# Last stage of a decoder layer: experts' residual through TensorE instead of through memory, and a new order of its small steps

## The reference, cut to what matters

```python
ff = h @ fc2_w + fc2_b                       # h = gelu(x @ fc1_w + fc1_b)
x = layernorm(x + ff, ln3_g, ln3_b)          # inside the cross-attention block
x = _layernorm(x_block_input + x)            # outer norm, called X4 below
# _L0_ffn_ref: tokens 0..15 of each sequence have an expert each, the others share one
xe = x[:, :16, :]
h = gelu(einsum('bnd,ndh->bnh', layernorm(xe, g_e, b_e), W1_e) + b1_e)
out_e = einsum('bnh,nhk->bnk', h, W2_e) + b2_e
out_s = gelu(layernorm(x[:, 16:, :], g_s, b_s) @ W1_s + b1_s) @ W2_s + b2_s
x = _layernorm(x + concatenate([out_e, out_s], axis=1))
```

## Time and profile before

| | us |
|---|---|
| median of 3 runs | 508.43 |
| lowest, highest | 505.97, 509.84 |
| the profiled execution, its own time | 509.53 |
| its span in the trace | 507.7 |
| TensorE, VectorE, ScalarE, POOL busy | 471.4, 384.4, 368.0, 252.4 |
| granted TensorE clock, mean over the span | 0.988 of full |

### The profile page before, as it was taken

One profiled execution on the slowest core, in us unless ns is written; L12 is line 12 of the kernel. 1 busy time (PEld: TensorE's weight loads), 2 busy tenths in 40 slices (PEclk: granted clock), 3 DMA queues, 4 the chain that ended last, 5 costly groups with the idle time before them and its releaser, 6 DMA issues.

```text
span 507.7 us, 14097 instructions
## 1 busy us (share of the span) xinstructions
PE 471.4 (93%) x4644; PEld 432.8 (85%) x4644; DVE 384.4 (76%) x1852; ACT 368.0 (72%) x1390; POOL 252.4 (50%) x342
## 2 busy tenths in 40 slices
PE   3779789999998989999999999999999999999894
PEld 3668788999998989999999999999999997798672
DVE  4667768888888887788878787777777777538866
ACT  4447886868688887777778887777777777836763
POOL 1453366656565665455444455554445545633432
PEclk9899999999999999999999999999999999999987
DMA  8740000000000004000000000000000000400003
GB/s 234 249 175 3 1 3 2 1 3 3 1 2 2 1 3 111 14 2 3 2 2 2 2 2 1 3 1 1 3 1 4 1 2 3 167 1 0 7 16 85
DMA packets 15720, 14.18 MB, mean 28 GB/s; under 512 B 2848, under 2 KB 13344, under 8 KB 15520
## 3 DMA queue, kind: packets, MB, share of 16 engines
q1 hardware_dynamic: 14080, 12.81, 8.0%
q10 hardware_dynamic: 1568, 0.47, 0.5%
HBM read 12.10 MB, written 1.18 MB: 26 GB/s over the span
## 4 chain that ended last, share of the span: by engine, by line
PE 77%; DVE 12%; issue 3%; POOL 2%; ACT 2%; DMA 2%; SPq 1%; POOLq 0%; DVEq 0%; ACTq 0%
PE late_bank L582 11%; PE late_bank L566 11%; PE late_bank L551 11%; PE late_bank L534 11%; PE late_bank L72 9%; PE late_bank L74 9%; PE late_bank L73 9%; DMA x<-in_xT 2%; DVE ffstats L1250 2%; PE late_bank L591 1%; DVE P L1078 1%; ACT P L817 1%; DVE N L1287 1%; PE late_bank L608 1%; DVE at_PT L1104 1%
## 5 line engine op out<-in xcount | busy, mean ns | idle before, releaser
L817 ACT ACTIVATE P<-P,at_negmax 128x128 f32<-128x128 f32 x512 | 199.8, 400 | 81.8 <-DVE at_negmax L1078 81.8
L1519 POOL TENSOR_TENSOR P<-P,at_inv 128x512 f32<-128x512 f32 x128 | 136.6, 1078 | 128.5 <-DVE at_inv L1088 128.4
L1104 DVE COPY at_PT<-late_bank 128x512 f32<-128x512 f32 x128 | 87.8, 688 | 36.0 <-PE late_bank L534 35.7
L1078 DVE CUSTOM_DVE_ANT_0 P<-late_bank,maskb 128x128 f32<-128x128 f32 x512 | 111.2, 286 | 1.8 <-PE late_bank L551 1.7
L817 ACT ACTIVATION_READ_ACCUMULATOR P<-P,at_negmax 128x1 f32 x512 | 101.9, 199 | 0.0
L534 PE MATMUL late_bank<-ident,P 128*128 128x128 f32 x512 | 76.4, 273 | 3.6 <-DVE at_negmax L1078 2.8
L534 PEld LDWEIGHTS late_bank<-ident,P 128*128 128x128 f32 x512 | 59.7, 140 | 9.8 <-issue 5.0
L551 PE MATMUL late_bank<-at_k,at_q 64*128 64x128 f32 x1024 | 65.8, 278 | 0.9 <-DVE at_k L1096 0.9
L551 PEld LDWEIGHTS late_bank<-at_k,at_q 64*128 64x128 f32 x1024 | 59.7, 188 | 4.8 <-issue 1.2
L566 PE MATMUL late_bank<-at_PT,V 128*64 128x128 f32 x1024 | 63.0, 276 | 0.0
L566 PEld LDWEIGHTS late_bank<-at_PT,V 128*64 128x64 f32 x1024 | 55.2, 137 | 3.9
(11 more groups left out here) (195 smaller groups left out, 1055.8 us busy)
## 6 DMA issues: line engine op xcount, KB each, us to landing
ctxT_raw<-in_ctxT SPq DMA_DIRECT2D x1, 1024.0 KB, 8.8
out<-xres SPq DMA_DIRECT2D x4, 224.0 KB, 2.5
x<-in_xT SPq DMA_DIRECT2D x1, 768.0 KB, 9.4
xres<-in_x SPq DMA_DIRECT2D x1, 768.0 KB, 13.6
tap_rows<-in_short_wT SPq DMA_DIRECT2D x3, 192.0 KB, 4.1
sa_wq_raw<-in_sa_wq SPq DMA_DIRECT2D x1, 512.0 KB, 8.0
sa_wk_raw<-in_sa_wk SPq DMA_DIRECT2D x1, 512.0 KB, 9.0
sa_wv_raw<-in_sa_wv SPq DMA_DIRECT2D x1, 512.0 KB, 9.8
```

The lines of the kernel that those rows point to most:

```text
L817: last = nc.scalar.activation(P[:, n % 2, h, :], P[:, n % 2, h, :], ACT.Exp, scale=-1.0, bias=negmax[:, n % 2, h:h + 1], accum_out=total[: ...
L1078: last = nc.vector.tensor_tensor_reduce(P[:, n % 2, h, :], score_bank(h), k.maskb[:, cols(n)], scale=1.0, scalar=3.0e38, op0=ALU.add, op1= ...
L1104: nc.vector.tensor_copy(PT[:, HQ * g:HQ * g + HQ, :], banks[T_BANK[g % 2]][:].rearrange("p (h l) -> p h l", h=HQ)).then_inc(pt_ok, 1)
L1519: nc.gpsimd.tensor_tensor(tile, tile, inv[:, n % 2, HQ * g:HQ * g + HQ].unsqueeze(2).to_broadcast([128, HQ, 128]), ALU.mult).then_inc(norm ...
```

## The change

The scratch tensor, its writes and its gathers go. In their place TensorE transposes the 16 expert tokens of each sequence of X4 (16 small transposes) into spare columns of the experts' bank, VectorE adds the experts' second bias (now loaded transposed, `b2_eT`) while it brings them to xE as features by (expert, sequence), and `experts_residual` puts them into bank E2: 16 matmuls with xE as stationary tile and the identity as moving one, before `experts_w2` accumulates on top. So `experts_second_bias`, the tile `select` and ScalarE's copy for it, and VectorE's sum go; the experts' statistics read the bank, and ScalarE instead of VectorE writes the experts' output, with a shift made by VectorE.

For the last group the residual of the feed-forward layer is put into the bank by TensorE (an identity matmul over xres) ahead of `fc2_sum`; VectorE's `residual_sum(3)` goes, and what follows reads the bank.

The orders: VectorE's `residual_sum(1)` and `(2)` stand before `inner_shift`; `experts_inputs` of each group stand before an `inner_shift` or `gained`; `outer_shift(3)` stands right behind z's rest. On TensorE the experts' first layer is split in two halves around `shared_w1(3)`, and `add_x4(2)`, `shared_w2(2)` stand behind `experts_w2`. ScalarE's `gelu_shared(3)` stands before `output_normal(0)`. SP stores groups 0 and 1, the four quadrants of experts, group 2, the last group; ScalarE's two stores of experts move to SP.

```diff
-    sp.dma_start(k.raw["bias2"][0:NEXP, :], io["b2_e"]).then_inc(k.ff_ld, 16)
-    row_broadcast(nc, sp, k.raw["bias2"][NEXP:128, :], io["b2_s"]).then_inc(k.ff_ld, 16)
+    sp.dma_start(k.experts_b2[:], io["b2_eT"]).then_inc(k.ff_ld, 16)
+    row_broadcast(nc, sp, k.raw["bias2"][:], io["b2_s"]).then_inc(k.ff_ld, 16)
...
-def fc2_sum(k, pe, g):
+def fc2_sum(k, pe, g, opened=False):
 
     pe.wait_ge(k.h_ok, 4 * (g + 1))
     for b in range(GRP):
         for c in range(FF // 128):
             last = k.nc.tensor.matmul(k.late_banks[FC2_BANK][:, b * 128:(b + 1) * 128], k.hT[g % 3][:, c, b, :],
-                                      k.fc2[:, c, :], start=(c == 0), stop=(c == FF // 128 - 1))
+                                      k.fc2[:, c, :], start=(c == 0 and not opened),
+                                      stop=(c == FF // 128 - 1 and (b == GRP - 1 or not opened)))
...
+        def experts_x4(g):
+            first = E1_X4 + g * GRP * NEXP if g < LAST else 0
+            return banks[E1_BANK if g < LAST else ZT_BANK][:, first:first + GRP * NEXP]
...
-            for g in range(NGRP):
-                sp.wait_ge(x4_ok, g + 1)
-                sp.dma_start(io["scratch"].rearrange("b n d -> n b d")[:, group(g), :],
-                             X4[0:NEXP, group(g), :]).then_inc(parked, 16)
-            sp.wait_ge(parked, 16 * NGRP)
-            sp.wait_ge(zeroed, 2)
-            for i in range(EQ):
-                sp.dma_start(xE[QUADRANT * i:QUADRANT * i + NSEQ],
-                             io["scratch"].rearrange("b (c i) d -> i b c d", i=EQ)[i]).then_inc(xe_in, 16)
-            for g in range(LAST):
+            for g in (0, 1):
                 store_group(sp, g)
             sp.wait_ge(ne_ok, 1)
-            for i in (0, 1):
+            for i in range(EQ):
                 store_experts(sp, i)
-            store_group(sp, LAST)
+            for g in (2, LAST):
+                store_group(sp, g)
...
             def next_fc2(g):
                 pe.wait_ge(r3_ok, g)
-                fc2_sum(k, pe, g)
+                if g == LAST:
+                    pe.wait_ge(res_ok, 2 * NSEQ)
+                    nc.tensor.matmul(banks[FC2_BANK][:], k.ident[:], k.xres[:, group(g), :], start=True, stop=False)
+                fc2_sum(k, pe, g, g == LAST)
...
-            def experts_w1():
+            def experts_w1(experts):
 
                 pe.wait_ge(ze_ok, NGRP)
                 pe.wait_ge(ld_w1e, 16)
                 pe.wait_ge(k.h_ok, 4 * NGRP)
-                for e in range(NEXP):
+                for e in experts:
...
-            def experts_second_bias():
-                pe.wait_ge(r3_ok, NGRP)
-                for part in (k.bias2.hi, k.bias2.lo):
-                    for c in range(NEXP // EQ):
-                        nc.tensor.matmul(banks[E2_BANK][:, c * 128:(c + 1) * 128],
-                                         k.select[0:NEXP, c].rearrange("e i s -> e (i s)"), part[0:NEXP, :],
-                                         start=(part is k.bias2.hi and c == 0), stop=False)
+            def x4_transposes(g):
+
+                pe.wait_ge(x4_ok, g + 1)
+                if g < LAST:
+                    pe.wait_ge(k.h_ok, 4 * NGRP)
+                else:
+                    pe.wait_ge(z_ok, NGRP)
+                for b in range(GRP):
+                    last = nc.tensor.transpose(experts_x4(g)[:, b * NEXP:(b + 1) * NEXP], X4[0:NEXP, g * GRP + b, :],
+                                               k.ident[0:NEXP, 0:NEXP])
+                last.then_inc(xe_mm, 1)
+
+            def experts_residual():
+                pe.wait_ge(gained_ok, NGRP)
+                pe.wait_ge(zeroed, 2)
+                pe.wait_ge(xe_ok, 2)
+                for c in range(NEXP // EQ):
+                    for i in range(EQ):
+                        nc.tensor.matmul(banks[E2_BANK][QUADRANT * i:QUADRANT * (i + 1), c * 128:(c + 1) * 128],
+                                         xE[:, (c * EQ + i) * NSEQ:(c * EQ + i) * NSEQ + QUADRANT], k.ident[:],
+                                         start=(c == 0), stop=False)
 
             def experts_w2():
                 pe.wait_ge(ld_w2e, 16)
-                pe.wait_ge(zeroed, 2)
...
             second_bias(2)
             shared_w2(1)
             shared_w1(2)
+            for g in range(LAST):
+                x4_transposes(g)
+            z_transposes(3)
             second_bias(3)
-            experts_second_bias()
+            experts_w1(range(0, 8))
+            shared_w1(3)
+            x4_transposes(3)
+            experts_w1(range(8, NEXP))
+            experts_residual()
+            experts_w2()
             add_x4(2)
-            z_transposes(3)
             shared_w2(2)
-            experts_w1()
-            shared_w1(3)
-            experts_w2()
             add_x4(3)
             shared_w2(3)
...
-                nc.scalar.activation(k.select[0:NEXP],
-                                     k.ident[0:NEXP, 0:NEXP].rearrange("e (c i) -> e c i", i=EQ).unsqueeze(3).to_broadcast(
-                                         [NEXP, NEXP // EQ, EQ, QUADRANT]), ACT.Copy).then_inc(k.bias_hi, 1)
...
+            def experts_output():
+                act.wait_ge(shift_e_ok, 1)
+                for c in range(NEXP // EQ):
+                    last = nc.scalar.activation(rE[:, c], banks[E2_BANK][:, c * 128:(c + 1) * 128], ACT.Identity,
+                                                bias=shift_e[:, c:c + 1], scale=rstd_e[:, c:c + 1])
+                last.then_inc(ne_ok, 1)
...
             z_affine(3)
+            gelu_shared(3)
             output_normal(0)
             gelu_experts()
-            gelu_shared(3)
             output_normal(1)
+            experts_output()
             output_normal(2)
-            act.wait_ge(ne_ok, 1)
-            for i in (2, 3):
-                store_experts(act, i)
...
+            def residuals(g):
+                return R3[:, g % 2] if g < LAST else quarter(FC2_BANK)
+
             def residual_moments(g):
-                vec.wait_ge(r3_ok, g + 1)
-                moments(g, 0, R3[:, g % 2])
+                if g < LAST:
+                    vec.wait_ge(r3_ok, g + 1)
+                else:
+                    vec.wait_ge(k.fc2_mm, g + 1)
+                moments(g, 0, residuals(g))
...
-                    last = nc.vector.scalar_tensor_tensor(N3[:, g % 2, b], R3[:, g % 2, b],
+                    last = nc.vector.scalar_tensor_tensor(N3[:, g % 2, b], residuals(g)[:, b],
...
-                vec.wait_ge(e1_mm, 1)
+                vec.wait_ge(e1_mm, 2)
...
-            def experts_sums():
+            def experts_inputs_x4(groups):
+
+                vec.wait_ge(xe_mm, groups[-1] + 1)
+                count = len(groups) * GRP
+                source = banks[E1_BANK if groups[0] < LAST else ZT_BANK][:, E1_X4 if groups[0] < LAST else 0:][:, 0:count * NEXP]
+                nc.vector.tensor_tensor(
+                    xE[:, 0:NEXP * NSEQ].rearrange("p (e b) -> p e b", e=NEXP)[:, :, groups[0] * GRP:groups[0] * GRP + count],
+                    source.rearrange("p (b e) -> p e b", e=NEXP),
+                    k.experts_b2[:].unsqueeze(2).to_broadcast([128, NEXP, count]), ALU.add).then_inc(xe_ok, 1)
+
+            def experts_statistics():
                 vec.wait_ge(e2_mm, 1)
-                vec.wait_ge(xe_in, 16 * EQ)
-                nc.vector.tensor_tensor(rE[:], quarter(E2_BANK), xE[:], ALU.add).then_inc(re_ok, 1)
-                vec.wait_ge(re_ok, 1)
                 for c in range(NEXP // EQ):
-                    last = nc.vector.bn_stats(stats_e[:, c], rE[:, c])
+                    last = nc.vector.bn_stats(stats_e[:, c], banks[E2_BANK][:, c * 128:(c + 1) * 128])
...
-            def experts_output():
+            def experts_shift():
                 vec.wait_ge(rstd_e_ok, 1)
-                for c in range(NEXP // EQ):
-                    last = nc.vector.tensor_scalar(rE[:, c], rE[:, c], mv_e[:, c, 0:1], rstd_e[:, c:c + 1],
-                                                   ALU.subtract, ALU.mult)
-                last.then_inc(ne_ok, 1)
+                nc.vector.scalar_tensor_tensor(shift_e[:], mv_e[:, :, 0], -1.0, rstd_e[:],
+                                               ALU.mult, ALU.mult).then_inc(shift_e_ok, 1)
...
             outer_sums(0)
+            residual_sum(1)
             inner_shift(0)
-            residual_sum(1)
             residual_moments(1)
             outer_shift(0)
             gained(1)
             outer_sums(1)
+            residual_sum(2)
             inner_shift(1)
-            residual_sum(2)
             residual_moments(2)
             outer_shift(1)
-            experts_inputs(0)
             gained(2)
             outer_sums(2)
-            residual_sum(3)
+            experts_inputs(0)
             inner_shift(2)
             residual_moments(3)
             outer_shift(2)
+            experts_inputs(1)
             gained(3)
-            experts_inputs(1)
             outer_sums(3)
```

(18 more changed lines are left out.)

24 lines of the change are left out of this document (12 added, 12 removed).

## The result

| | before | after |
|---|---|---|
| median of 4 runs, us | 508.56 | 514.51 |
| lowest, highest | 505.97, 509.84 | 513.47, 517.11 |
| the profiled execution, its own time | 509.53 | 513.59 |
| its span | 507.7 | 511.8 |
| granted TensorE clock, mean | 0.988 | 0.979 |

The ratio of after to before is 1.0128, with a 95% interval of 1.0078 to 1.0178: about 6 us slower. I had forecast 508.9 us and a range of 504.5 to 513.0. The time lies above the range, at rival 2 (514.8 us, chance 0.12).

A forecast was written before the change was run, and what follows sets the result against it. TensorE was taken to bound the end: 487.0+10.8+3.4 = 501.2, then an unchanged 4.02 us, +0.43; with small terms +0.5 us. Forecast: 510.0 profiled, 508.9 us median, range 504.5 to 513.0.

The forecast's parts named there:

- rival 2: Last stage: narrow and 32-column matmuls hold the clock low from 488.4 to the end, +6.4, 514.8 us; chance 0.12.
- the part on the clock: TensorE's tail: as much low-clock time as before, 6.8 us, costing half of itself, 3.4 us.
- Rival 1: Last stage: the clock stays at full, TensorE ends at 497.8, -2.9, 505.6 us; chance 0.18.
- Rival 3: Experts' bias or gelu slips, so their second layer waits: up to 1.5 us, 510.4 us; chance 0.08.
- VectorE's half: VectorE's reordering in the last 50 us: last z transposes start 2.5 us sooner, experts' first layer 4.1 sooner.
- step (c): Group 3's feed-forward residual added by TensorE ahead of fc2(3) instead of by VectorE: costs 0.2 us.
- (a): VectorE's residual_sum(1) and (2) ahead of inner_shift, into idle time: group 2's statistics start 1.13 us sooner.
- (b): VectorE's experts_inputs(0) moved into the wait for POOL: group 2's statistics to outer_sums(2) takes 2.64 us, not 3.04.
- TensorE's half: TensorE's work behind 487.0: 10.8 us at full clock, bounds 10.2 to 12.6.
- wait of about 1 us for bias and gelu: A wait of about 1 us in TensorE's tail before the change, now covered by experts_residual.
- The copy's removal itself is worth nothing: The experts' copy through memory isn't on the chain: gathers land by 496.1, their use starts at 498.60.
- The end: From group 3's statistics to the last output: 4.02 us, unchanged; SP's stores add 0 to 0.3, taken as 0.1.

The follow-up runs named there:

- e8: The changed kernel with six throw-away narrow matmuls (16 columns, two passes each) in TensorE's gap ahead of the last z transposes: 513.83 us, ratio 1.011.
- e4: The kernel before with VectorE's new order alone, the residual still through memory and TensorE's order as before: 505.66 us, ratio 0.9943.
- e15: The kernel before with VectorE's new order and the last group's feed-forward residual added by TensorE, the experts' residual still through memory: 504.64 us, ratio 0.9941.
- e5: The changed kernel with group 2's add_x4 and shared_w2 back in the gap and add_x4(3) between the halves of the experts' first layer: 508.63 us, ratio 1.0024.
- e3: The changed kernel without the experts' residual and second bias, both left out of the computation: 515.36 us, ratio 1.015.
- e9: The changed kernel with group 2's wide work back in the gap and without the experts' residual and second bias: 509.74 us, ratio 1.0033.
- the three pairs: Three kernels, each timed with inputs in new and old memory places: ratios 1.0128 and 1.0104, 1.0035 and 0.9999, 0.9985 and 0.9943.
- e18: Word-for-word repeat: the kernel before with VectorE's new order and the last group's residual by TensorE: 505.73 us, ratio 0.9967.
- e12: Word-for-word repeat: the kernel before with VectorE's new order alone: 505.39 us, ratio 0.9949.

## Why the prediction was wrong

**The failed step** is in the part on the clock: "I take as much low time as before, which costs half of itself, 3.4". The low time was 13.7 us and cost 6.8. That is 3.4 more than I had, of the 3.6 us between my 510.0 for the profiled execution and the 513.59 measured; the start-up's 0.8 more and some 0.6 less in small terms make up the rest. With group 2's work back in the hole (e1) the low time was 3.4 us, with throw-away wide matmuls in it (e2) 6.8. I had seen that group 2's second layer left the place ahead of the experts, and booked it only as work moved behind. I hadn't asked what the hole does that it leaves: 1.67 us in which TensorE stands still, with narrow matmuls behind it. My own sum had no work for TensorE between some 484 and 485.9. My reasons for as much low time as before named the narrow matmuls that stay and are added and the wide ones that move to the end, and not what is missing where those stood.

**Rival 2** gave the time (514.8) and named the point, that group 3's first layer would have to bring the clock back. It didn't: 2.06 us at half clock (L658 at 491.76), and the clock stayed low. But it had the fall at 488.4; it came at 486.56 in the gap, and the return at 500.22 within the experts' second layer, not at the end. Its chance of 0.12 was too small: against it I set that the clock "came back at 498.68 behind much this mix". In that mix group 3's wide first layer stood directly ahead of the experts' second layer:

```profile
494.93 1.74 PE L657 MATMUL late_bank<-zT,w1s 128*128 128x512 f32 x2
496.60 1.94 PE L707 MATMUL late_bank<-w2e,hE 128*32 128x128 f32 x32
```

The change puts the second narrow half of 3.5 us between them, and it takes group 2's second layer out of the stretch of 488.5 to 491.8, where the clock first came back. That rival 2's time agrees to 0.3 us is in part luck: its low stretch was to last 18.8 us and lasted 13.7, and the fall in the gap and the start-up's 0.8 us, which it didn't have, made up for some of it. **Rival 1** (full clock, 505.6) didn't come, and the rule of the Trainium skill beside it doesn't account for e8 (above). **Rival 3** (bias and gelu late) didn't come: VectorE waited for the experts' first layer 1.83 us, not the other way round:

```profile
497.92 0.42 DVE L1387 TENSOR_TENSOR hE_in<-late_bank,b_raw 128x256 f32<-128x256 f32 x1 [1.83 <-PE late_bank L690]
```

**VectorE's half** came out as forecast. Counted from the first ffR sum (456.85 before, 457.67 after), the last group's statistics gained 22.40-21.02 = 1.38 us (forecast 1.35), outer_sums(3) 1.25 (1.15), the last z transposes 2.66 (2.5):

```profile
478.69 0.88 DVE L1270 BATCH_NORM_STATS2 ffstats<-late_bank 128x6 f32<-128x128 f32 x4
...
480.57 1.12 DVE L1302 SCALAR_TENSOR_TENSOR N<-late_bank,ffmv,ln_g 128x128 f32<-128x128 f32 x4
481.73 1.14 DVE L1313 SCALAR_TENSOR_TENSOR N<-N,ffrstd,x 128x128 f32<-128x128 f32 x4
```

Two small terms within it were off. Reading PSUM cost nothing in `gained` (1.12 us against 1.14 from SBUF; I took +0.2). And step (c) gains 0.2 in the trace instead of costing 0.2: e4, which has (a) and (b) alone, took 21.22 us to the same statistics, e15 21.03. The experts' first layer began 3.5 us sooner (30.73 us after the first ffR sum, 34.21 before), not 4.1, since transposes and bias ahead of it ran at half clock.

**TensorE's half.** I had 10.8 us of full-clock work. Measured: from 488.40 to 504.61, 16.21 us, of which 11.8 up to 500.22 at half clock, so 11.8/2+4.4 = 10.3. The count was good; 16 matmuls of the residual took 1.94 us at half clock and 1.08 at full clock in e5 (taken 1.2). The "wait of about 1 us for bias and gelu" that I saw in the kernel before wasn't there: TensorE was busy with group 3's first layer up to the start of L707 (the two rows above). It stands in no term of the sum. Such a wait comes only with the split, 1.06 us in e3 and e9, where no residual fills it. "The copy's removal itself is worth nothing" held: e4, which keeps the copy and pulls the experts forward, lost nothing to it. Its sum at 494.56 waited only 0.21 us, and by the profile for TensorE.

**The end** held: from group 3's statistics to the end of the last output 3.99 us (4.02), and SP's six last stores cost 0.3 us more behind it (I took 0.1 of 0 to 0.3).

**The start-up** wasn't in the prediction. I had written that the loop and what lies ahead of it stay as they are; in the profiled execution it cost the 0.8 us by which the last stage began late, about 1.7 us by the three pairs, as likely as these are.

## What to carry to other kernels

When an edit moves wide matmuls away from between narrow ones, work out what TensorE does in the hole, and look at the granted clock by stretch before pricing the work at full speed: here putting the moved work back into the hole won 5 us, and throw-away wide matmuls in it won 4. Make an order of small steps on its own first: VectorE's order alone, a part of this change, beat the kernel before by 0.5% (505.4 to 505.7 us), and what was added to it beyond the last group's residual gave that back. Where single traces disagree, as they do here, the mean clock of every execution tells how much of a difference the clock can be. If code that wasn't touched runs later after a change, compare where the inputs lie in memory.

## What I hadn't expected of the hardware

- A TensorE 100% busy stayed at 1.2 GHz for 13 us (487 to 500) in after; most of its matmuls there had 16 moving columns or stationary tiles of 32.
- Six matmuls of 512 columns and six of 16 (in two passes each) took nearly the same 1.66 and 1.51 us in the same gap, and left low stretches of 6.8 and 10.2 us.
- Loads ran at 342 to 358 GB/s or at 396 to 403 GB/s from 10 to 15 us, by where the inputs lay in memory.
- Word for word the same kernel showed no low stretch under TensorE's last stage in one profiled execution (e15) and 6.8 us in another (e18).
- The same kernel began its last stage at 457.07 us in one profiled execution (e4) and at 455.80 in another (e12). The clock differed in the start-up, 0.79 and 1.00 from 15 to 20 us (3.4 us at 1.2 GHz in e4, none in e12), so a single trace tells a stage's length, but not the place of its start to better than a microsecond.
